# Fused adaLN layer (linear attention, then routed experts): the q, k and v projections in fp16 halves

## The reference

```python
h = layernorm(x) * (1 + ca) + sa          # x: [2, 2048, 256]
q, k, v = relu(h @ Wq.T + bq), relu(h @ Wk.T + bk), h @ Wv.T + bv
s = gamma * s + outer(k_t, v_t); z = gamma * z + k_t      # a scan over 2048 tokens
y_t = (q_t @ s) / (sum(q_t * z) + EPS)
x = x + ga * y
h = layernorm(x) * (1 + cb) + sb
e = argmax(h @ Wr.T + br)                 # one of 8 experts for each token
x = x + gb * (relu(h @ W1[e].T + b1[e]) @ W2[e].T + b2[e])
```

## Time and profile before

| | |
|---|---|
| median of 3 runs | 466.65 us (466.51 to 466.78) |
| the profiled execution | 469.77 us, its span 467.5 us |
| PE busy | 439.2 us (94%) |
| DVE busy | 385.9 us (83%) |
| ACT busy | 305.1 us (65%) |
| POOL busy | 260.2 us (56%) |
| mean granted PE clock | 0.977 |

### The profile page before, as it was taken

The page is one execution under the profiler, slowest core; times in us unless marked ns, Lnnn a source line. Parts: engine busy times, 40 slices in busy tenths (PEclk is TensorE's granted clock), DMA queues, the critical chain, the costliest instruction groups (busy, mean ns, idle before and its releaser), DMA issues.

```text
span 467.5 us, 13656 instructions
## 1 busy us (share of the span) xinstructions
PE 439.2 (94%) x4296; PEld 392.0 (84%) x4296; DVE 385.9 (83%) x1012; ACT 305.1 (65%) x804; POOL 260.2 (56%) x429
## 2 busy tenths in 40 slices
PE   7999999999999999995767999999999999999992
PEld 4898889999889988893436999989999999999991
DVE  2548999999999999999985887787887777888862
ACT  1335666666666666664606877878777888778870
POOL 2112577777667766756346465656656556664332
PEclk9999999999999999997779999999999999999997
DMA  8725344444444444411015243443333443442110
GB/s 281 254 81 175 119 159 158 158 158 153 152 147 153 156 157 147 136 47 68 25 32 141 59 104 76 110 100 88 87 85 90 87 116 78 97 58 57 45 29 2
DMA packets 43572, 51.71 MB, mean 111 GB/s; under 512 B 24811, under 2 KB 37356, under 8 KB 41328
## 3 DMA queue, kind: packets, MB, share of 16 engines
q1 hardware_dynamic: 37552, 36.67, 27.1%
q0 software_dynamic: 4992, 12.60, 9.8%
q10 hardware_dynamic: 960, 1.57, 1.0%
HBM read 35.22 MB, written 13.50 MB: 104 GB/s over the span
## 4 chain that ended last, share of the span: by engine, by line
PE 76%; DVE 13%; issue 3%; DMA 3%; DVEq 2%; ACT 1%; POOL 1%; ACTq 0%; POOLq 0%
PE ps_o L1434 17%; PE ps_qk L1351 11%; PE ps_qk L1420 9%; PE ps_va L1420 9%; PE ps_va L1361 6%; PE ps_o L1310 5%; PE ps_kv L1317 5%; PE ps_va L1338 3%; PE ps_o L1306 3%; DVE w L1123 2%; DMA w<-in_wmod 2%; DVE arena L1109 2%; PE ps_k L1189 2%; DVEq L1127 1%; PE ps_x L1231 1%
## 5 line engine op out<-in xcount | busy, mean ns | idle before, releaser
L1434 PE MATMUL ps_o<-w,arena 128*128 x936 | 108.7, 273 | 0.6 <-DVE arena L1109 0.4
L1434 PEld LDWEIGHTS ps_o<-w,arena 128*128 128x128 f16 x936 | 89.8, 98 | 10.9 <-issue 1.2
L1123 DVE COPY w<-w 128x2048 f16 x78 | 59.2, 760 | 34.5 <-PE ps_va L1420 23.9
L660 ACT ACTIVATE arena<-ps_qk,arena 128x128 f32<-128x128 f32 x156 | 44.6, 368 | 41.9 <-PE ps_qk L1420 39.1
L1351 PE MATMUL ps_qk<-arena,wqk_b 128*128 128x128 f32 x512 | 62.4, 275 | 0.0
L1420 PE MATMUL ps_qk<-arena,w 128*128 128x128 f16 x936 | 58.7, 219 | 3.6 <-DVE w L1123 1.9
L544 POOL DMA_INDIRECT out_rows<-arena,slot_token x39 | 42.1, 1081 | 34.5 <-POOL arena L540 30.6
L1351 PEld LDWEIGHTS ps_qk<-arena,wqk_b 128*128 128x128 f32 x512 | 59.7, 192 | 0.0
L1420 PEld LDWEIGHTS ps_qk<-arena,w 128*128 128x128 f16 x936 | 55.2, 98 | 5.3 <-issue 2.4
L1420 PE MATMUL ps_va<-arena,w 128*128 128x128 f16 x936 | 58.6, 219 | 0.2 <-DVE w L1123 0.2
L1109 DVE TENSOR_TENSOR arena<-arena 128x512 f16<-128x512 f32 x78 | 53.3, 683 | 4.7 <-ACT arena L668 3.7
(11 more groups left out here) (192 smaller groups left out, 834.2 us busy)
## 6 DMA issues: line engine op xcount, KB each, us to landing
w<-in_w_raw SPq DMA_DIRECT2D x16, 1024.0 KB, 5.1
token_rows<-arena SPq DMA_DIRECT2D x64, 128.0 KB, 1.9
arena<-in_x SPq DMA_DIRECT2D x32, 128.0 KB, 2.1
b_sb<-in_b2b SPq DMA_DIRECT2D x1, 1024.0 KB, 5.3
w<-in_wmod ACTq DMA_DIRECT2D x1, 768.0 KB, 8.7
w<-in_wqkv SPq DMA_DIRECT2D x1, 768.0 KB, 8.1
arena<-token_rows,slot_token POOLq DMA_INDIRECT x39, 3.6
out_rows<-arena,slot_token POOLq DMA_INDIRECT x39
```

The lines of the kernel that those rows point to most:

```text
L660: last = act.activation(hid[:, f, :], bank[("qk", "va")[h]][:, (f % 4) * P:(f % 4 + 1) * P], ACT.Relu, bias=consts_now[:, r, f:f + 1], sca ...
L1123: dve.tensor_copy(now[:, :, i * F // 2:(i + 1) * F // 2], of[:, :, i * F // 2:(i + 1) * F // 2]).then_inc(s_w1, 1)
L1434: last = pe.matmul(bank[f"o{n % 2}"][:, 0:D], hid_parts[:, r % 2, b, f, :], w[:, bass.ds(m, 1), a, f * D:(f + 1) * D].rearrange("p a d -> ...
```

## The change

q, k and v are computed from fp16 halves. The transposed item is kept as two fp16 tiles: the upper half is x times 1024, rounded (ACT, as before but with a scale), the lower half the rest (DVE, h_lo, new, in each slot between lo_piece and scale_matrix). The weights are scaled by a power of two, found on the chip from a bound on their size, and kept as two halves too. Each fp32 product becomes three fp16 ones: upper by upper, upper by lower, lower by upper. The power of two is taken out again in the decay matrix, in the constant added to the denominator, in the biases and at L994.

In the head DVE gets qk_bound, qk_scales, h_lo for item 0, qk_lo for each batch row, v_scales and v_lo for each batch row; router_columns moves ahead of slot (0, 0) and gets a reduction over v's weights. PE gets two products with a matrix of ones, which sum a bound over the lanes, and does router_through_v between the bias sums of q and those of k. ACT's upper halves of the q and k weights now wait for qk_scales, and it also makes the upper halves of v's weights. POOL loses two memsets.

```diff
-        wqk_b = sb("wqk_b", [P, B, 2, DK, D])
+        wqk_b = sb("wqk_b", [P, B, 2, 2, DK, D], F16)
...
-        h_t = cut(B, DK, P)
+        h_t = cut(B, DK * P).bitcast(F16).rearrange("p b (i k t) -> p b i k t", i=2, k=DK)
...
-        wv_b = cut(B, DK, DV)
+        wv_b = cut(B, DK * DV).bitcast(F16).rearrange("p b (i k c) -> p b i k c", i=2, k=DK)
...
-                    act.activation(h_t[:, r], bank["x"][:, 0:D].rearrange("p (k t) -> p k t", k=DK),
-                                   ACT.Copy).then_inc(s_ht, 1)
+                    act.activation(h_t[:, r, 0], bank["x"][:, 0:D].rearrange("p (k t) -> p k t", k=DK),
+                                   ACT.Copy, scale=X_ONE).then_inc(s_hhs, 1)
...
-                    act.wait_ge(s_modt_ready, 1)
+                    act.wait_ge(s_ss, 1)
                     for h in range(DK):
-                        last = act.activation(wqk_b[:, u, :, h, :], wqkv_sb[:, 0:2, h, :], ACT.Copy,
-                                              scale=scale_at[:, h, u:u + 1])
-                    last.then_inc(s_wqk, 1)
+                        last = act.activation(wqk_b[:, u, 0, :, h, :], wqkv_sb[:, 0:2, h, :], ACT.Copy,
+                                              scale=scale_qk[:, h, u:u + 1])
+                    last.then_inc(s_whq, 1)
+                if (k, u) == (-1, 1):
+                    act.wait_ge(s_sv, 1)
+                    for b in range(B):
+                        act.activation(wv_b[:, b, 0], wv_f[:, b], ACT.Copy, scale=v_scale).then_inc(s_whv, 1)
...
+                dve.wait_ge(s_qks, 1)
+                step(dve.tensor_scalar(qk_sum, bank["kv0"][:, 0:1], 2.0 ** -20, None, ALU.max))
...
+            def qk_bound():
+                dve.wait_ge(s_wqkv, 32)
+                dve.tensor_reduce(qk_most[:, 0:1], wqkv_sb[:, 0:2].rearrange("p m h d -> p (m h d)"), AX_X, ALU.max,
+                                  apply_absolute_value=True)
+                dve.wait_ge(s_modt_ready, 1)
+                step(dve.tensor_reduce(qk_most[:, 1:2], scale_at, AX_XY, ALU.max, apply_absolute_value=True))
+                dve.tensor_tensor(qk_most[:, 0:1], qk_most[:, 0:1], qk_most[:, 1:2], ALU.mult).then_inc(s_qkm, 1)
+
+            def power_of_two(largest, scale, whole, back):
+
+                step(dve.tensor_scalar(head_bits.bitcast(I32), largest.bitcast(I32), EXPONENT, None, ALU.bitwise_and))
+                step(dve.tensor_scalar(scale.bitcast(I32), head_bits.bitcast(I32), -1.0, float((TOP + 254) * EXP_ONE),
+                                       ALU.mult, ALU.add))
+                dve.tensor_scalar(back.bitcast(I32), head_bits.bitcast(I32), float(-(TOP + 10) * EXP_ONE), None, ALU.add)
+                step(dve.tensor_scalar(whole, scale, X_ONE, None, ALU.mult))
+
+            def qk_scales():
+                power_of_two(qk_sum, qk_scale, qk_all, qk_back)
+                dve.tensor_scalar(scale_qk[:], scale_at, qk_scale, None, ALU.mult).then_inc(s_ss, 1)
+                dve.tensor_scalar(decay[:], decay[:], qk_back, qk_back, ALU.mult, ALU.mult).then_inc(s_decayed, 1)
+
+            def qk_lo(b):
+                dve.wait_ge(s_whq, b + 1)
+                for h in range(DK):
+                    last = dve.scalar_tensor_tensor(wqk_b[:, b, 1, :, h, :], wqkv_sb[:, 0:2, h, :],
+                                                    scale_qk[:, h, b:b + 1], wqk_b[:, b, 0, :, h, :], ALU.mult,
+                                                    ALU.subtract)
+                last.then_inc(s_wqk, 1)
+
+            def v_scales():
+                dve.wait_ge(s_wvs, 1)
+                step(dve.tensor_scalar(v_sum, bank["o0"][:, 0:1], 2.0 ** -20, None, ALU.max))
+                power_of_two(v_sum, v_scale, v_all, v_back)
+                dve.memset(scales[:, 15:16], 0.0).then_inc(s_sv, 1)
+                dve.tensor_scalar(den_eps, v_all, DEN_EPS, None, ALU.mult)
+                dve.wait_ge(s_init, INIT)
+                dve.tensor_copy(v_ext[:, :, DX:DZ], v_all.unsqueeze(1).to_broadcast([P, B, 1]))
+
+            def v_lo(b):
+                dve.wait_ge(s_whv, b + 1)
+                dve.scalar_tensor_tensor(wv_b[:, b, 1], wv_f[:, b], v_scale, wv_b[:, b, 0], ALU.mult,
+                                         ALU.subtract).then_inc(s_wvb, 1)
+
+            def h_lo(k, u):
+                if it := att_item(k, u, XPOSE):
+                    n, g, r = it
+                    dve.wait_ge(s_hhs, n + 1)
+                    dve.scalar_tensor_tensor(h_t[:, r, 1], bank["x"][:, 0:D].rearrange("p (k t) -> p k t", k=DK),
+                                             X_ONE, h_t[:, r, 0], ALU.mult, ALU.subtract).then_inc(s_ht, 1)
...
+                step(dve.tensor_copy(of_width[:, :, :, DX:DV], u_t[:]))
+                step(dve.tensor_reduce(v_most[:, 0:1], wv_f.rearrange("p b h c -> p (b h c)"), AX_X, ALU.max,
+                                       apply_absolute_value=True))
+                dve.memset(scales[:, 14:15], 0.0).then_inc(s_wvm, 1)
...
                 if (k, u) == (-1, 0):
+                    qk_bound()
                     router_scale()
+                    qk_scales()
+                    router_centre()
                     v_weights(0)
-                    router_centre()
                     v_weights(1)
+                    h_lo(-1, 1)
+                    qk_lo(0)
+                    router_columns()
                     projection_biases()
+                    v_scales()
+                    v_lo(0)
+                    qk_lo(1)
+                    v_lo(1)
                     b1_bound()
...
-                    dve.tensor_scalar(den[:, r, 0:1], o[:, DX:DZ], DEN_EPS, None, ALU.add).then_inc(s_den, 1)
+                    dve.tensor_scalar(den[:, r, 0:1], o[:, DX:DZ], den_eps, None, ALU.add).then_inc(s_den, 1)
...
-                    dve.tensor_scalar(x_sb[:, r, g % 4, D:DX], bank["va"][:, DX:DV], rs1[:, g % 2, r, 3:4], None,
-                                      ALU.mult).then_inc(s_xe, 1)
+                    dve.tensor_scalar(x_sb[:, r, g % 4, D:DX], bank["va"][:, DX:DV], rs1[:, g % 2, r, 3:4], v_back,
+                                      ALU.mult, ALU.mult).then_inc(s_xe, 1)
...
                     lo_piece(k, u, 1 if k < FULL else 0)
+                h_lo(k, u)
...
+            pe.wait_ge(s_qkm, 1)
+            pe.matmul(bank["kv0"][:, 0:1], con("ones"), qk_most[:, 0:1], start=True, stop=True).then_inc(s_qks, 1)
             keep_busy("o1", 4)
...
             for m in range(3):
+                if m == 1:
+                    router_through_v()
...
+                    if n == 0:
+                        pe.wait_ge(s_wvm, 1)
+                        pe.matmul(bank["o0"][:, 0:1], con("ones"), v_most[:, 0:1], start=True, stop=True).then_inc(s_wvs, 1)
                     for m in range(2):
                         for c in range(DK):
-                            for h in range(DK):
-                                last = pe.matmul(bank["qk"][:, (m * DK + c) * P:(m * DK + c + 1) * P],
-                                                 wqk_b[:, r, m, h, c * P:(c + 1) * P], h_t[:, r, h, :],
-                                                 start=(h == 0), stop=(h == DK - 1))
+                            for q, (a, b) in enumerate(PARTS):
+                                for h in range(DK):
+                                    last = pe.matmul(bank["qk"][:, (m * DK + c) * P:(m * DK + c + 1) * P],
+                                                     wqk_b[:, r, a, m, h, c * P:(c + 1) * P], h_t[:, r, b, h, :],
+                                                     start=(q == 0 and h == 0), stop=(q == 2 and h == DK - 1))
                     last.then_inc(s_qkp, 1)
-                    if n == 0:
-                        router_through_v()
-                        pe.wait_ge(s_wvb, 1)
+                    need(pe, s_wvb, min(n + 1, B))
                     need(pe, s_att, n)
                     need(pe, s_xe, n)
-                    for h in range(DK):
-                        last = pe.matmul(bank["va"][:, 0:DV], h_t[:, r, h, :], wv_b[:, r, h, :],
-                                         start=(h == 0), stop=(h == DK - 1))
+                    for q, (a, b) in enumerate(PARTS):
+                        for h in range(DK):
+                            last = pe.matmul(bank["va"][:, 0:DV], h_t[:, r, b, h, :], wv_b[:, r, a, h, :],
+                                             start=(q == 0 and h == 0), stop=(q == 2 and h == DK - 1))
                     last.then_inc(s_vp, 1)
```

More of the change, by code:

```diff
@@ L1232, in transpose_x, with router_through_v @@
                 last.then_inc(s_xt, 1)
+            def router_through_v():
+                pe.wait_ge(s_gu, 1)
+                pe.wait_ge(s_wvr, 16)
+                for c in range(DK):
+                    for h in range(DK):
+                        last = pe.matmul(wide(bank["o1"], c * B * NE, B * NE), wv_rows_sb[:, h, c * P:(c + 1) * P],
```

(3 more changed lines are left out.)

43 lines of the change are left out of this document (23 added, 20 removed).

## The result

The changed kernel takes 480.12 us in the median of 4 runs (476.49 to 481.33), beside 466.71 for the kernel before in the same comparison (4 runs, 466.51 to 469.45): 1.026 times as long, 95% interval 1.019 to 1.033. It is slower than the kernel before, by more than the forecast of 474.5 and inside the range of 467.5 to 483. The profiled execution took 480.75 us, span 478.7, 11.2 more than before.

A forecast was written before the change was run, and what follows sets the result against it. The prediction took PE to bound the attention stage at 5.94 us per item, against DVE's own 5.63. Head 3.0 plus stage 4.9 gave 7.9 us, put on the median of 466.65 for 474.5 us; range 467.5 to 483.

The forecast's parts named there:

- DVE becomes the bound: Attention stage: PE falls from 5.94 to 5.28 us per item, DVE needs 6.02 without waits for GpSimd.
- Rival (4): Attention stage: DVE's row is elastic and a quicker PE pulls the other engines along; 453.5 us at the extreme, chance 0.05.
- 6.12 us per item: Attention stage: DVE's pace with h_lo and 0.10 us of waits, +0.18 over 27 slots, +4.9 us.
- DVE's own work, 5.63: Attention stage before the change: 5.95 us per item less 0.32 of waits for GpSimd.
- The edits at L947 and L994: Attention stage, DVE: a scalar from SBUF for an immediate, or a second multiply in the same pass, costs nothing.
- L989's wait should close, L880's stay: Attention stage, DVE's waits for GpSimd: 0.23 us per item closes as DVE arrives 0.39 later, 0.10 stays.
- Rival (1): Attention stage: all waits for GpSimd stay, 6.34 us per item, 480.5 us in all; chance 0.22.
- Head +3.0: Head: serial DVE work that PE waits for delays item 1 by 3.5 us, 0.5 given back; bounds +1.5 to +4.5.
- rival (2): Head: the clock falls to 1.2 GHz as PE waits, about 8 us more, 482.5 us in all; chance 0.10.
- signs given for a wrong prediction: h_lo takes other than 0.4 us or waits for ACT, or the head moves item 1 by under 1.5 or over 5 us.
- The drain, "nothing": After k = 15, with no projection and no h_lo, the time doesn't change.
- correction to the median: Whole kernel: the profiled 469.77 us lies 3.1 above the median of 466.65, so the difference goes on the median.

The follow-up runs named there:

- e6: Changed kernel with PE leaving out, for q, k and v, the product of the weights' lower half with the item's upper half; 478.39 us, ratio 1.024.
- e3: Changed kernel with h_lo's instruction issued twice per item, the first into a tile that nobody reads; 491.53 us, ratio 1.054.
- e5: Changed kernel with two scalars read from SBUF, for the denominator's constant and the second factor, put back as immediates; 476.14 us, ratio 1.018.
- e8: e7 with the router's columns also moved from DVE to ACT and their factor to POOL; 473.04 us, ratio 1.0125.
- e4: Kernel before with only h_lo's instruction added, into a tile PE doesn't read but waits for; 474.49 us, ratio 1.015.
- e7: Changed kernel with e1's fillers and, from item 1 on, v's bias added by PE and v copied by ACT instead of DVE; 475.38 us, ratio 1.017.
- e10: e1 with 5 more filler products before PE's wait for item 0's v; 477.33 us, ratio 1.0225.
- e9_after_again: The changed kernel itself run once more, unedited, with another profile; 478.99 us, ratio 1.025 to the kernel before.
- e1: Changed kernel with 14 fp16 filler products on PE in two waits of the head; 478.59 us, ratio 1.027.

## Why the prediction was right, and where it was not

**DVE becomes the bound: right, and shown.** PE lost 0.67 us per item where 0.66 was predicted (1.79 to 1.34 and 0.92 to 0.70), its busy time over items 4 to 30 is 142.11 / 26 = 5.47 us per item (5.28 was predicted for the work alone; the record of a group ahead of a gap counts 0.16 us more than the time to the next start in an unbroken row: 1.50 beside 1.34 for L1440), and less work on PE changed nothing (e6: 6.15) while more on DVE cost at least its whole length (e3: 6.63). Rival (4), that a quicker PE pulls DVE along, is excluded by the same two runs, although its condition, 0.4 us of waits in the 5.95, turns out to be met (below). In the chain of the work that ended last DVE's share went from 13% to 38% of the span, PE's from 76% to 44%.

**6.12 us per item: 6.16 measured, and so close partly by luck, as four terms were off and offset one another.** h_lo was priced at 0.39 us from L960 and takes 0.33. The step that failed is the choice of the row. L960 (L1040 after the change, still 0.40) reads its scalar from SBUF, which h_lo doesn't. A nearer row was there, L1000, which like h_lo reads PSUM and one SBUF operand and no scalar from SBUF:

```profile
105.02 0.42 DVE L1000 TENSOR_TENSOR arena<-ps_va,bias_v 128x264 f32<-128x264 f32 x1
105.36 0.74 DVE L880 SCALAR_TENSOR_TENSOR w<-w,w_scale 128x512 f16<-128x512 f32 x1
```

It gives way after 0.34 us, for 264 columns, with fp32 in and out, so neither fp32 nor the operand in SBUF makes the difference of 0.06 to L960. What is left is the scalar, and 0.06 is what one costs in e5; on L960 itself that wasn't tried. The edits at L947 and L994, "nothing", are 0.06 us each; e5 shows that they count. L994 "already has one such scalar", and a second one costs again.

The fourth term is DVE's own work, 5.63. It leaves out three lines of the router's choice, each run once in eight items, that were stretched too. One of them between 60 and 190 us in the kernel before:

```profile
L916 DVE TENSOR_TENSOR chosen<-pick 128x64 f16<-128x64 f32 x2 | 1.6, 780 | 0.0
```

The other two, L909 and L912, are at 633 and 558 ns there; after the change the three are at 408, 362 and 191. Against the shortest durations seen (403, 184, 186) the kernel before waited (377 + 449 + 372) ns x 2 / 26 = 0.09 us per item in them. So 0.41 and not 0.32 of its 5.95 us were waits and its own work was 5.54. In the sum, 0.09 and 0.06 too much for own work and h_lo stand against 0.12 too little for the two edits and 0.06 too little for the waits that stayed (next paragraph).

**"L989's wait should close, L880's stay": right as a reading, by rows.** L1069 is at 244 ns and L953 at 766, so 0.055 + 0.09 = 0.14 us of waits are left in these two lines, of 0.32, where I took 0.10 (with the router's choice 0.16 of 0.41). The Trainium skill (SBUF — State Buffer, Who interferes with whom) has a DVE instruction with two SBUF inputs and a GpSimd one that reads SBUF block each other, and a DVE instruction with at most one SBUF input, outside its 2-port modes, go free. The traces agree: h_lo takes 408 to 425 ns over its 32 instances, while L1086 in e8 is stretched to 650 and ends (126.22 + 0.65) with POOL's L492 (126.12 + 0.73). Rival (1), all waits stay, is excluded for the changed kernel. That DVE's later arrival is what closes L989's wait is shown in part only: in e4, where h_lo makes DVE as much later, the line is still at 309 ns. Yet with every wait closed e4 would have been at 5.63 + 0.33 = 5.96 and was at 6.20. Of the difference 0.18 are waits still to be seen, (309 - 189) + 2 x (750 - 722) ns, and the other 0.06 are those of the router's choice, at 354, 499 and 724 ns in e4. The same waits opening again make up what e7 and e8 fell short by, together with h_lo's wait for ACT in e8. Why they don't close further when DVE sets the pace, and open when it is relieved, has not been settled; no run here moves or removes GpSimd's work.

**Head +3.0: right for the work, wrong for the clock.** With the clock kept full (e10) item 4 comes 3.2 us late and item 1 at 32.94 instead of 33.0. In the changed kernel's two profiles it was +7.4 and +7.3, because rival (2) happened beside the forecast and not instead of it. The prediction gave them as alternatives, 0.50 and 0.10, though nothing kept them apart; this step failed. Its price was too high as well: 8 us were forecast, 4.2 measured (e10 against after), of which 2 are made up after item 30 in that pair, and e3 and e5 show executions with the same head that pay 1 us or nothing.

**Its own signs.** Two of the signs given for a wrong prediction came: h_lo takes 0.33 and not 0.4 us, and item 1 moved by 7.7 us, more than 5. A third came once: h_lo waited 1.1 us for ACT before one of its 32 instances. The signs for a right one came too, but for item 1: gaps on PE, L1440 at 1.34 us, DVE without idle time, L1027 every 6.13 us, L1069 at 0.24.

**The drain, "nothing": -1.0 us.** The kernel before had the clock at 0.50 from 217.0 to 227.2 and from 237.4 to 244.2 us, 17 us in all, the one after for 10.2; that fits a quicker drain, and the runs don't take it apart further.

**The base.** On the profiled executions the forecast was 469.77 + 7.9 = 477.7 against 480.75, 3.1 us short. The other 2.5 of the miss come from the correction to the median: the execution profiled before lay 3.1 above its median, the one after 0.6. The granted clock of the executions shows what stands behind such differences. In the nine executions of the changed kernel (four of the comparison, five of e9_after_again), the three at a mean clock of 0.969 took 480.75, 480.93 and 481.33 us, and the one at 0.980 took 476.49. The kernel before lay between 465.9 and 470.34 us in 17 executions, at 0.977 to 0.985. My sentence that this kernel's runs lie within 0.03% rested on three of them.

So the forecast's mechanism held and its own range, 470.5 to 478.5, did not: the median is 480.12, close to rival (1)'s 480.5, and not for rival (1)'s reason. That the wider range of 467.5 to 483 holds it is owed to the room left for the rivals. Open: what decides whether the head's low stretch lasts 13.65 us (both profiles of the changed kernel) or 3.4 (e3 and e5, with the same head, and e6, with fewer products in it).

## What to carry to other kernels

When an edit trades work on a full engine for work on another that is full too, add up the second one first: here 0.67 us per item taken from PE bought nothing, and 0.45 put on DVE was paid at 0.19. Time that an engine spends waiting inside its durations is not free room: 0.33 us of new work found only 0.1 of it. Nor is work taken off that engine all gain: of 0.34 us in e7, 0.27 came back as waits. To find such waits, compare the mean of every line with its shortest, the seldom ones too. If a change makes PE wait for a microsecond or two in the head, a slower clock is to be added to the forecast, with a chance, and not kept as an alternative, and its cost is to be read over the whole span and from several executions.

## What the runs showed of the hardware

A scalar read from SBUF in place of an immediate makes a small DVE instruction 61 ns longer: 207 against 146 ns for 128x1 from PSUM, 276 against 215 for 128x8 that already has one such scalar. The start of the next instruction moves as much (122.53 - 122.41 = 0.12 us after L1027, 0.07 in e5).

The granted clock fell to 0.50 in the head after a stretch in which PE was busy 2.62 of 4.5 us, with one wait of 1.88 us in it, and in e1 after one with PE busy 2.76 of 3.8 us and a wait of 1.04; it then stayed there for 13.65 us in the changed kernel, with PE busy 12.69 of 13.5, and for 3.4 us in e1. After the same 2.62 of 4.5 us with a wait of 1.88 the clock stayed full in e3, and after a wait of 1.03 us it stayed full in e8: the same work on PE is followed by a fall in one execution and not in another.

Waits for GpSimd lie inside DVE's durations: a 128x8 instruction with two inputs in SBUF took 189 ns at its shortest and up to 700, one of 128x256 with an input in PSUM 408 to 425.
